# GRU chunks without zeroing: reset and keep inputs in a chunk's first step, candidate scan into PSUM

## The chip, the cores and the metric

The kernel runs on one core of a Trainium2 chip. The metric is the device time of one execution in microseconds (us), as the median of several runs. TensorE is called PE here, its weight loads PEld, VectorE is DVE, ScalarE is ACT, GpSimd is POOL.

## The reference

The network has four layers on an input of 8 x 16 x 16 x 96: a spectral mixing layer with an MLP, a Toeplitz layer, and two GRU layers (L2 and L3). The change concerns the GRU layers only. Each of them runs four independent GRUs (two sums of a forward and a reverse direction) over the 256 positions of the image, for 8 batch elements, with 96 hidden units. The recurrence cannot be split over the positions:

```python
def step(hprev, gxt):                 # gx = x @ wih.T + bih for all positions beforehand
    gh = hprev @ whh.T + bhh
    r = jax.nn.sigmoid(gxt[:, :h] + gh[:, :h])
    z = jax.nn.sigmoid(gxt[:, h:2 * h] + gh[:, h:2 * h])
    n = jnp.tanh(gxt[:, 2 * h:] + r * gh[:, 2 * h:])
    hn = (1.0 - z) * n + z * hprev
    return (hn, hn)
...
fwd = _bigru(x_inner, f_wih_fw, f_whh_fw, ...)
bwd = jnp.flip(_bigru(jnp.flip(x_inner, 1), b_wih_fw, b_whh_fw, ...), 1)
y = jax.nn.silu(fwd + bwd) * jax.nn.silu(z)
```

## The kernel before

`gru_steps` runs the 256 steps of a layer; it is called once for L2 and once for L3. The four GRUs form two groups g = 0 and 1 of two GRUs each (j = 0, 1); a group's state is 96 partitions (hidden units) by 16 columns (2 GRUs x 8 batch elements, `PER`). The loop over steps q does group 0 and then group 1 on every engine, so one group's step is a **half step**, and the two groups take turns. Every engine works through its own list in the order in which the code writes it; semaphores tie the lists together.

The state is kept as fp32 (`states`), and for PE as two fp16 parts, `h_hi` (rounded) and `h_lo` (the rest); the weights are two fp16 parts as well. A half step on PE is 12 small matmuls with `h_hi` (4 for each of the gates RESET, CAND, KEEP) and 6 with `h_lo` (2 for each gate), each with 8 moving columns. They add into PSUM sums that already hold the input's part.

Steps go in chunks of 8 (`STEPS`), 32 chunks a layer. The input's part of a gate, for all 8 steps of a chunk, takes 6 matmuls of 64 columns, called **products** here (`inputs`, line 1087, run at line 1105). Before the change the products of the next chunk are spread over the steps of the current one (`ahead`): one RESET and one KEEP product in six of the steps 1 to 7, six CAND products over all 8. RESET and KEEP have one bank for each group, which holds two chunks' regions (p = 0, 1), so the region of the next chunk is zeroed first, by ACT, in the first step of a chunk (lines 1077 and 1078), for 30 of the 32 chunks; the products then add onto zeros. CAND has a bank for each p, and its first product clears the bank (start=True).

A half step on the other engines: ACT takes the sigmoid of the RESET sum (line 1072), of the KEEP sum (`keep`, 1074), and of its negative (`renew`, 1075); in a chunk's first step it then writes the zeros. DVE's scan (1022, `cand`) computes input plus r times the hidden part; ACT takes its tanh (1081); DVE multiplies keep and the old state (1029, `kept_part`), and a scan gives the new `h_hi` (1037) and another one the fp32 state (1039), from which `h_lo` comes (1045, `rest`). DVE's list for one half step of group 0 is

```python
candidate(0, q)
rest(1, q - 1)
kept_part(0, q)
new_state(0, q)      # h_hi, then states
```

and for group 1 the same with the groups changed: the `h_lo` of one group stands behind the candidate of the other one.

## Time and profile before

| | |
|---|---|
| median of 3 runs | 1226.55 us (1225.07 to 1228.66) |
| the profiled execution | 1223.94 us |
| its span, first to last instruction | 1222.1 us |
| PE, DVE, ACT busy | 1081.0, 943.3, 777.5 us |
| granted TensorE clock, mean of the span | 0.585 |
| steps of L2, first to last candidate scan | 297.22 to 722.75 us |
| steps of L3, first to last candidate scan | 772.11 to 1197.45 us |

The profile counts matmuls as busy while they overlap, so that PE's busy time is not its work. The steps of the two GRU layers hold 851 us of the span. A granted clock of 1.0 is 2.4 GHz, 0.5 is 1.2 GHz.

### The profile page before, as it was taken

How to read it: one execution, taken by the hardware profiler on the slowest of the kernel's cores; microseconds unless marked ns; L12 is line 12 of the kernel's file. 1: busy time of each engine (PE TensorE's matmuls, PEld its weight loads, DVE VectorE, ACT ScalarE, POOL GpSimd, SP SyncE). 2: the span in 40 equal slices, each digit the busy share in tenths (PEclk: the TensorE clock that was granted, in tenths of full speed). 3: DMA queues.
4: the chain of work that ended last, by engine and by line, in shares of the span. 5: the costliest groups of instructions: out<-in, count | busy, mean ns of one | idle time of the engine just before them, and what ended most of it. 6: DMA issues, size and time to landing. Idle time of an engine off the chain costs nothing. (4 is left out here: it accounts for less than half of the span.)

```text
span 1222.1 us, 57375 instructions
## 1 busy us (share of the span) xinstructions
PE 1081.0 (88%) x22390; PEld 854.9 (70%) x22390; DVE 943.3 (77%) x5701; ACT 777.5 (64%) x4509; POOL 113.1 (9%) x94
## 2 busy tenths in 40 slices
PE   3787799858999999999999968999999999999996
PEld 2555254344888888888888855688888888888885
DVE  3544799984888888888888885688888888888886
ACT  4224620007777777777777764777777777777773
POOL 1001389910000000000000000000000000000000
PEclk8588899957555555555555557555555555555555
DMA  4000500000000000000000000000000000000000
GB/s 119 2 1 12 131 1 1 1 5 2 4 4 4 4 4 4 4 4 4 3 4 4 4 3 5 3 4 4 3 4 4 4 4 3 4 4 4 4 3 27
DMA packets 8234, 12.71 MB, mean 10 GB/s; under 512 B 5745, under 2 KB 7121, under 8 KB 7674
## 3 DMA queue, kind: packets, MB, share of 16 engines
q1 hardware_dynamic: 7962, 9.05, 2.9%
q8 instruction: 175, 2.87, 1.0%
q14 instruction: 97, 0.79, 0.2%
HBM read 8.26 MB, written 0.79 MB: 7 GB/s over the span
## 5 line engine op out<-in xcount | busy, mean ns | idle before, releaser
L1037 DVE TENSOR_TENSOR_SCAN L2s_h_hi<-L2s_renew,L2s_terms 96x32 f16<-96x32 f32 x512 | 112.9, 221 | 74.4 <-ACT L2s_terms L1081 16.0
L1037 DVE TENSOR_TENSOR_SCAN L3s_h_hi<-L3s_renew,L3s_terms 96x32 f16<-96x32 f32 x512 | 113.0, 221 | 74.4 <-ACT L3s_terms L1081 16.0
L1129 PE MATMUL L2s_reset_sum<-L2s_h_hi,L_w_hidden 97*128 97x8 f16 x2048 | 141.0, 179 | 20.8 <-DVE L2s_h_hi L1037 8.4
L1129 PE MATMUL L3s_reset_sum<-L3s_h_hi,L_w_hidden 97*128 97x8 f16 x2048 | 141.1, 179 | 20.6 <-DVE L3s_h_hi L1037 7.8
L1129 PEld LDWEIGHTS L3s_reset_sum<-L3s_h_hi,L_w_hidden 97*128 97x128 f16 x2048 | 94.6, 107 | 78.6 <-DVE L3s_h_hi L1037 31.5
L1129 PEld LDWEIGHTS L2s_reset_sum<-L2s_h_hi,L_w_hidden 97*128 97x128 f16 x2048 | 94.6, 107 | 78.6 <-DVE L2s_h_hi L1037 32.0
L1072 ACT ACTIVATE L3s_reset<-L3s_reset_sum 96x16 f32<-96x16 f32 x512 | 93.0, 182 | 65.8 <-PE L3s_reset_sum L1129 5.1
L1072 ACT ACTIVATE L2s_reset<-L2s_reset_sum 96x16 f32<-96x16 f32 x512 | 93.0, 182 | 65.7 <-PE L2s_reset_sum L1129 4.6
L1081 ACT ACTIVATE L2s_terms<-L2s_cand 96x16 f32<-96x16 f32 x512 | 111.0, 217 | 30.1 <-DVE L2s_cand L1022 3.5
L1129 PE MATMUL L3s_keep_sum<-L3s_h_hi,L_w_hidden 97*128 97x8 f16 x2048 | 130.0, 174 | 0.0
L1129 PE MATMUL L2s_keep_sum<-L2s_h_hi,L_w_hidden 97*128 97x8 f16 x2048 | 130.0, 174 | 0.0
L1129 PE MATMUL L3s_cand_sum<-L3s_h_hi,L_w_hidden 97*128 97x8 f16 x2048 | 130.0, 174 | 0.0
L1129 PE MATMUL L2s_cand_sum<-L2s_h_hi,L_w_hidden 97*128 97x8 f16 x2048 | 130.0, 174 | 0.0
L1081 ACT ACTIVATE L3s_terms<-L3s_cand 96x16 f32<-96x16 f32 x512 | 111.0, 217 | 29.6 <-DVE L3s_cand L1022 2.4
L1129 PE MATMUL L2s_reset_sum<-L2s_h_lo,L_w_hidden 96*128 96x8 f16 x1024 | 114.1, 185 | 0.8 <-DVE L2s_h_lo L1045 0.2
L1129 PE MATMUL L3s_reset_sum<-L3s_h_lo,L_w_hidden 96*128 96x8 f16 x1024 | 114.2, 185 | 0.7 <-DVE L3s_h_lo L1045 0.3
L1022 DVE TENSOR_TENSOR_SCAN L2s_cand<-L2s_reset,L2s_cand_sum 96x32 f32<-96x32 f32 x512 | 109.8, 214 | 3.0 <-ACT L2s_reset L1072 1.1
L1129 PE MATMUL L2s_keep_sum<-L2s_h_lo,L_w_hidden 96*128 96x8 f16 x1024 | 112.1, 183 | 0.0
L1129 PE MATMUL L3s_keep_sum<-L3s_h_lo,L_w_hidden 96*128 96x8 f16 x1024 | 112.1, 183 | 0.0
L1022 DVE TENSOR_TENSOR_SCAN L3s_cand<-L3s_reset,L3s_cand_sum 96x32 f32<-96x32 f32 x512 | 109.8, 214 | 2.8 <-ACT L3s_reset L1072 1.1
L692 DVE SCALAR_TENSOR_TENSOR l_acc<-l_v,coef,l_acc 96x384 f32<-96x384 f32 (+11 forms) x88 | 103.6, 1241 | 0.4
L1129 PE MATMUL L3s_cand_sum<-L3s_h_lo,L_w_hidden 96*128 96x8 f16 x1024 | 102.8, 174 | 0.0
(251 smaller groups left out, 3415.2 us busy)
## 6 DMA issues: line engine op xcount, KB each, us to landing
L_wih_raw<-in_L_wih SPq DMA_DIRECT2D x2, 1152.0 KB, 11.6
l_w_raw<-in_L_w SPq DMA_DIRECT2D x1, 1296.0 KB
L_w_hidden_raw<-in_L_whh SPq DMA_DIRECT2D x2, 576.0 KB
stream<-in_x SPq DMA_DIRECT2D x2, 384.0 KB, 3.7
out<-stream SPq DMA_DIRECT2D x4, 192.0 KB, 2.1
l_idft<-in_idft SPq DMA_DIRECT2D x1, 400.0 KB
rpe_lw<-in_rpe_lw SPq DMA_DIRECT2D x1, 384.0 KB
l_dft<-in_dft SPq DMA_DIRECT2D x1, 288.0 KB, 3.0
```

Of the source, the lines that this page charges most:

```text
L692: e.scalar_tensor_tensor(out=row(to, acc), in0=row(of, v), scalar=coef[:, m, axis, at:at + 1], in1=row(to, acc), op0=ALU.mult, op1=ALU.add ...
L1022: e.tensor_tensor_scan(flat(cand[g][:, x]), flat(reset[g][:, x]), flat(cand_sum(g, p)[0:C, :, :, s]), 0.0, ALU.mult, ALU.add).then_inc(can ...
L1037: e.tensor_tensor_scan(flat(h_hi[g][0:C, x]), flat(renew[g][:, x]), flat(terms[g][:, x]), 0.0, ALU.mult, ALU.add).then_inc(hi_ready[g], 1)
L1072: e.activation(reset[g][:, x, :, 1], reset_sum(g, p)[0:C, :, s], ACT.Sigmoid).then_inc(activated[g], 1)
L1081: e.activation(terms[g][:, x, :, 0], cand[g][:, x, :, 1], ACT.Tanh).then_inc(activated[g], 1)
L1129: return e.matmul(dst, weights.hidden[0:rows, wp, GATES * (2 * g + j) + gate, :], rhs, start=False, stop=False, skip_group_check=True)
```

## The change

The zeroing is gone, and with it the buffer `zeros`. RESET and KEEP use one region of their bank. All 6 RESET products and all 6 KEEP products of a chunk are run in the chunk's own first step, among the matmuls of the state; the first of each six has start=True and clears the bank's flags, so that the others and the state's matmuls write or add as is due. The KEEP matmuls with `h_hi` move behind the RESET and CAND matmuls with `h_lo`, in every step. The six CAND products of the next chunk stay spread over the steps. The candidate scan writes its result to a free part of the CAND bank in PSUM instead of SBUF, and the tanh reads it there.

```diff
-        cand = pairs("cand", [C, 2, PER, 2])
...
-        zeros = sb("zeros", [C, PER, STEPS])
...
-        reset_sum = lambda g, p: reset_bank[g][:, p]
-        keep_sum = lambda g, p: keep_bank[g][:, p]
+        reset_sum = lambda g, p: reset_bank[g][:, 0]
+        keep_sum = lambda g, p: keep_bank[g][:, 0]
...
+        cand = lambda g, p, x: cand_bank[g][p][0:C, 2].rearrange("p c s -> p (c s)")[:, x * 2 * PER:(x + 1) * 2 * PER]
...
-                    e.tensor_tensor_scan(flat(cand[g][:, x]), flat(reset[g][:, x]), flat(cand_sum(g, p)[0:C, :, :, s]), 0.0,
+                    e.tensor_tensor_scan(cand(g, p, x), flat(reset[g][:, x]), flat(cand_sum(g, p)[0:C, :, :, s]), 0.0,
                                          ALU.mult, ALU.add).then_inc(cand_ready[g], 1)
...
-                    renewed = s == 0 and 1 <= q // STEPS < CHUNK_COUNT - 1
...
-                        if renewed:
-                            e.activation(reset_sum(g, 1 - p)[0:C], zeros[:], ACT.Copy)
-                            e.activation(keep_sum(g, 1 - p)[0:C], zeros[:], ACT.Copy)
...
-                        e.activation(terms[g][:, x, :, 0], cand[g][:, x, :, 1], ACT.Tanh).then_inc(activated[g], 1)
+                        e.activation(terms[g][:, x, :, 0], cand(g, p, x).rearrange("p (c k) -> p c k", k=2)[:, :, 1], ACT.Tanh).then_inc(activated[g], 1)
...
-                            first = j == 0 and (wp, xp) == (0, 0) and (gate == CAND or chunk == 0)
+                            first = j == 0 and (wp, xp) == (0, 0)
...
-                        def ahead(gate, first):
-                            if following < CHUNK_COUNT:
-                                for product in share(inputs(g, gate, following), s, first):
-                                    run(product)
-
-                        e.wait_ge(hi_ready[g], q + 1)
-                        for gate in (RESET, CAND, KEEP):
+                        def high(gate):
                             for j in range(2):
                                 add(gate, 0, 0, j)
                                 add(gate, 1, 0, j)
-                        ahead(RESET, 1)
+
+                        e.wait_ge(hi_ready[g], q + 1)
+                        resets, keeps = (inputs(g, RESET, q // STEPS), inputs(g, KEEP, q // STEPS)) if s == 0 else ([], [])
+                        for product in resets[:1]:
+                            run(product)
+                        high(RESET)
+                        for product in resets[1:]:
+                            run(product)
+                        high(CAND)
 
                         e.wait_ge(lo_ready[g], q + 1)
                         add(RESET, 0, 1, 0)
                         add(RESET, 0, 1, 1).then_inc(reset_summed[g], 1)
                         add(CAND, 0, 1, 0)
                         add(CAND, 0, 1, 1).then_inc(cand_summed[g], 1)
-                        ahead(KEEP, 1)
+                        for product in keeps[:1]:
+                            run(product)
+                        high(KEEP)
+                        for product in keeps[1:]:
+                            run(product)
                         add(KEEP, 0, 1, 0)
                         add(KEEP, 0, 1, 1).then_inc(keep_summed[g], 1)
-                        ahead(CAND, 0)
+                        if following < CHUNK_COUNT:
+                            for product in share(inputs(g, CAND, following), s):
+                                run(product)
```

The order of PE's matmuls in a half step. `L2s_h_hi` and `L2s_h_lo` are the state's parts, `L_forward` is the input (its rows are the products), and x4 means four such matmuls in a row. In the first step of chunk 1 (step 8), group 0, PE has before the change:

```order
L1129 MATMUL L2s_reset_sum<-L2s_h_hi,L_w_hidden 128x8 x4
L1129 MATMUL L2s_cand_sum<-L2s_h_hi,L_w_hidden 128x8 x4
L1129 MATMUL L2s_keep_sum<-L2s_h_hi,L_w_hidden 128x8 x4
L1129 MATMUL L2s_reset_sum<-L2s_h_lo,L_w_hidden 128x8 x2
L1129 MATMUL L2s_cand_sum<-L2s_h_lo,L_w_hidden 128x8 x2
L1129 MATMUL L2s_keep_sum<-L2s_h_lo,L_w_hidden 128x8 x2
L1105 MATMUL L2s_cand_sum<-L_forward,L_w_input 128x8x8
```

and after it, at the same place:

```order
L1101 MATMUL L2s_reset_sum<-L_forward,L_w_input 128x64
L1122 MATMUL L2s_reset_sum<-L2s_h_hi,L_w_hidden 128x8 x4
L1101 MATMUL L2s_reset_sum<-L_forward,L_w_input 128x64 x5
L1122 MATMUL L2s_cand_sum<-L2s_h_hi,L_w_hidden 128x8 x4
L1122 MATMUL L2s_reset_sum<-L2s_h_lo,L_w_hidden 128x8 x2
L1122 MATMUL L2s_cand_sum<-L2s_h_lo,L_w_hidden 128x8 x2
L1101 MATMUL L2s_keep_sum<-L_forward,L_w_input 128x64
L1122 MATMUL L2s_keep_sum<-L2s_h_hi,L_w_hidden 128x8 x4
L1101 MATMUL L2s_keep_sum<-L_forward,L_w_input 128x64 x5
L1122 MATMUL L2s_keep_sum<-L2s_h_lo,L_w_hidden 128x8 x2
L1101 MATMUL L2s_cand_sum<-L_forward,L_w_input 128x8x8
```

Twelve products have moved into this half step, six of them ahead of the `h_lo` matmuls of RESET and six between those and the last KEEP matmul. In another step (step 7, group 1) there stands before:

```order
L1129 MATMUL L2s_reset_sum<-L2s_h_hi,L_w_hidden 128x8 x4
L1129 MATMUL L2s_cand_sum<-L2s_h_hi,L_w_hidden 128x8 x4
L1129 MATMUL L2s_keep_sum<-L2s_h_hi,L_w_hidden 128x8 x4
L1105 MATMUL L2s_reset_sum<-L_forward,L_w_input 128x64
L1129 MATMUL L2s_reset_sum<-L2s_h_lo,L_w_hidden 128x8 x2
L1129 MATMUL L2s_cand_sum<-L2s_h_lo,L_w_hidden 128x8 x2
L1105 MATMUL L2s_keep_sum<-L_forward,L_w_input 128x64
L1129 MATMUL L2s_keep_sum<-L2s_h_lo,L_w_hidden 128x8 x2
L1105 MATMUL L2s_cand_sum<-L_forward,L_w_input 128x8x8
```

and after:

```order
L1122 MATMUL L2s_reset_sum<-L2s_h_hi,L_w_hidden 128x8 x4
L1122 MATMUL L2s_cand_sum<-L2s_h_hi,L_w_hidden 128x8 x4
L1122 MATMUL L2s_reset_sum<-L2s_h_lo,L_w_hidden 128x8 x2
L1122 MATMUL L2s_cand_sum<-L2s_h_lo,L_w_hidden 128x8 x2
L1122 MATMUL L2s_keep_sum<-L2s_h_hi,L_w_hidden 128x8 x4
L1122 MATMUL L2s_keep_sum<-L2s_h_lo,L_w_hidden 128x8 x2
L1101 MATMUL L2s_cand_sum<-L_forward,L_w_input 128x8x8
```

The RESET and KEEP products have left, and the four KEEP matmuls with `h_hi` have moved from ahead of the `h_lo` matmuls to behind four of them. On ACT the first step of chunk 1, group 0, is before:

```order
L1072 ACTIVATE L2s_reset<-L2s_reset_sum 96x16
L1074 ACTIVATE L2s_keep<-L2s_keep_sum 96x16
L1075 ACTIVATE L2s_renew<-L2s_keep_sum 96x16
L1077 ACTIVATE L2s_reset_sum<-L2s_zeros 96x128
L1078 ACTIVATE L2s_keep_sum<-L2s_zeros 96x128
L1081 ACTIVATE L2s_terms<-L2s_cand 96x16
```

and after, with the next half step's first operation:

```order
L1071 ACTIVATE L2s_reset<-L2s_reset_sum 96x16
L1073 ACTIVATE L2s_keep<-L2s_keep_sum 96x16
L1074 ACTIVATE L2s_renew<-L2s_keep_sum 96x16
L1077 ACTIVATE L2s_terms<-L2s_cand_sum 96x16
L1071 ACTIVATE L2s_reset<-L2s_reset_sum 96x16
```

The two zeroing writes between `renew` and the tanh are gone, and the tanh reads the CAND bank.

## Rows read from the trace of the kernel before

**Rows 1.** The page: engine PE over the span, and the granted clock in 40 slices.

```profile
PE 1081.0 (88%) x22390; PEld 854.9 (70%) x22390; DVE 943.3 (77%) x5701; ACT 777.5 (64%) x4509; POOL 113.1 (9%) x94
...
PEclk8588899957555555555555557555555555555555
```

**Rows 2.** Busy time by window, the steps of L2; columns PE, PEld, DVE, ACT, POOL, clock.

```profile
310.00:720.00 410.00, 389.66 (x9944) 331.97 (x9942) 335.27 (x2461) 319.13 (x2089) 0.00 (x0) 0.50 0.02 4
```

**Rows 3.** Timeline, one ordinary half step: start us, duration us, engine, line, operation.

```profile
438.75 0.22 DVE L1022 TENSOR_TENSOR_SCAN L2s_cand<-L2s_reset,L2s_cand_sum 96x32 f32<-96x32 f32 x1
...
438.88 0.15 DVE L1045 TENSOR_TENSOR L2s_h_lo<-L_states,L2s_h_hi 96x16 f16<-96x16 f32 x1
...
439.00 0.22 ACT L1081 ACTIVATE L2s_terms<-L2s_cand 96x16 f32<-96x16 f32 x1
...
439.09 0.22 PE L1129 MATMUL L2s_reset_sum<-L2s_h_lo,L_w_hidden 96*128 96x8 f16 x2
...
439.25 0.22 DVE L1037 TENSOR_TENSOR_SCAN L2s_h_hi<-L2s_renew,L2s_terms 96x32 f16<-96x32 f32 x1
439.35 0.18 ACT L1072 ACTIVATE L2s_reset<-L2s_reset_sum 96x16 f32<-96x16 f32 x1
439.39 0.19 DVE L1039 TENSOR_TENSOR_SCAN L_states<-L2s_renew,L2s_terms 96x32 f32<-96x32 f32 x1
...
439.52 0.27 PE L1129 MATMUL L2s_reset_sum<-L2s_h_hi,L_w_hidden 97*128 97x8 f16 x4
439.56 0.22 DVE L1022 TENSOR_TENSOR_SCAN L2s_cand<-L2s_reset,L2s_cand_sum 96x32 f32<-96x32 f32 x1
...
439.86 0.21 PE L1105 MATMUL L2s_reset_sum<-L_forward,L_w_input 97*128 97x64 f16 x1
...
439.90 0.22 PE L1129 MATMUL L2s_reset_sum<-L2s_h_lo,L_w_hidden 96*128 96x8 f16 x2
```

**Rows 4.** Timeline of DVE: two candidate scans twelve half steps apart within a chunk.

```profile
446.24 0.22 DVE L1022 TENSOR_TENSOR_SCAN L2s_cand<-L2s_reset,L2s_cand_sum 96x32 f32<-96x32 f32 x1
...
456.00 0.22 DVE L1022 TENSOR_TENSOR_SCAN L2s_cand<-L2s_reset,L2s_cand_sum 96x32 f32<-96x32 f32 x1
```

**Rows 5.** Timeline, DVE and ACT, the first step of a chunk.

```profile
443.63 0.22 DVE L1022 TENSOR_TENSOR_SCAN L2s_cand<-L2s_reset,L2s_cand_sum 96x32 f32<-96x32 f32 x1
443.66 0.28 ACT L1077 ACTIVATE L2s_reset_sum<-L2s_zeros 96x128 f32<-96x128 f32 x1
...
444.06 0.21 ACT L1081 ACTIVATE L2s_terms<-L2s_cand 96x16 f32<-96x16 f32 x1
...
444.45 0.19 DVE L1039 TENSOR_TENSOR_SCAN L_states<-L2s_renew,L2s_terms 96x32 f32<-96x32 f32 x1
...
444.56 0.19 DVE L1022 TENSOR_TENSOR_SCAN L2s_cand<-L2s_reset,L2s_cand_sum 96x32 f32<-96x32 f32 x1
...
445.43 0.22 DVE L1022 TENSOR_TENSOR_SCAN L2s_cand<-L2s_reset,L2s_cand_sum 96x32 f32<-96x32 f32 x1
```

**Rows 6.** Groups by line and form: count, busy us, mean ns of one.

```profile
L1081 ACT ACTIVATE L2s_terms<-L2s_cand 96x16 f32<-96x16 f32 x512 | 111.0, 217 | 30.1 <-DVE L2s_cand L1022 3.5
...
L1072 ACT ACTIVATE L2s_reset<-L2s_reset_sum 96x16 f32<-96x16 f32 x512 | 93.0, 182 | 65.7 <-PE L2s_reset_sum L1129 4.6
```

**Rows 7.** Timeline of PE in the steps: two small matmuls, product, two small, product.

```profile
440.79 0.20 PE L1129 MATMUL L2s_cand_sum<-L2s_h_lo,L_w_hidden 96*128 96x8 f16 x2
440.84 0.21 PE L1105 MATMUL L2s_keep_sum<-L_forward,L_w_input 97*128 97x64 f16 x1
440.87 0.23 PE L1129 MATMUL L2s_keep_sum<-L2s_h_lo,L_w_hidden 96*128 96x8 f16 x2
440.95 0.21 PE L1105 MATMUL L2s_cand_sum<-L_forward,L_w_input 97*128 97x64 f16 x1
```

**Rows 8.** Timeline of PE, six products in a row before the first step.

```profile
294.73 0.34 PE L1105 MATMUL L2s_reset_sum<-L_forward,L_w_input 97*128 97x64 f16 x6 [0.94 <-PEq L892]
294.91 0.34 PE L1105 MATMUL L2s_cand_sum<-L_forward,L_w_input 97*128 97x64 f16 x6
```

More of the change, by code:

```diff
@@ L993, in gru_steps @@
         updated, hi_ready, lo_ready = each("updated"), each("hi_ready"), each("lo_ready")
-        PREPARED = 2 + 7 * GROUPS
+        PREPARED = 1 + 7 * GROUPS
         with nc.Block() as block:
@@ L1001, in _ @@
                 e.memset(warm[:], 0.0).then_inc(prepared, 1)
-                e.memset(zeros[:], 0.0).then_inc(prepared, 1)
                 for g in range(GROUPS):
@@ L1105, in run, with share @@
                     return e.matmul(dst, lhsT, rhs, start=start, stop=False, skip_group_check=True)
-                def share(products, s, first):
-                    if s < first:
-                        return []
-                    n, steps = len(products), STEPS - first
-                    return products[round((s - first) * n / steps):round((s - first + 1) * n / steps)]
+                def share(products, s):
+                    n = len(products)
+                    return products[round(s * n / STEPS):round((s + 1) * n / STEPS)]
                 for g in range(GROUPS):
-                    for gate in (RESET, CAND, KEEP):
-                        for product in inputs(g, gate, 0):
-                            run(product)
+                    for product in inputs(g, CAND, 0):
+                        run(product)
                 e.wait_ge(prepared, PREPARED)
@@ L1130, in add @@
                                             start=False, stop=False, skip_group_check=True)
-                        def ahead(gate, first):
-                            if following < CHUNK_COUNT:
-                                for product in share(inputs(g, gate, following), s, first):
-                                    run(product)
-                        e.wait_ge(hi_ready[g], q + 1)
-                        for gate in (RESET, CAND, KEEP):
+                        def high(gate):
                             for j in range(2):
@@ L1148, in _ @@
                         add(CAND, 0, 1, 1).then_inc(cand_summed[g], 1)
-                        ahead(KEEP, 1)
+                        for product in keeps[:1]:
[3 more added lines that the diff above has]
+                            run(product)
                         add(KEEP, 0, 1, 0)
                         add(KEEP, 0, 1, 1).then_inc(keep_summed[g], 1)
-                        ahead(CAND, 0)
+                        if following < CHUNK_COUNT:
+                            for product in share(inputs(g, CAND, following), s):
+                                run(product)
 def gru_output(nc, layer, stream, gate, states, w_out, w_loaded, stats, out_dram, stored):
```

## The prediction

> **What bounds the kernel now.** I read the page first: PE is busy 1081.0 of 1222.1 us, and its granted clock is 5 tenths through nearly all of the steps [rows 1]. The window over L2's steps says the same, 389.66 of 410 us busy at 0.50, that is the 1.2 GHz level [rows 2]. That looks like a kernel bound by PE, but matmuls overlap in the profile, so I went to the timeline of one half step [rows 3] and asked what each engine waits for.
>
> A chain closes there. The candidate scan starts at 438.75; `h_lo` of the other group stands right behind it, 438.88 to 439.03; PE starts its two RESET matmuls with `h_lo` at 439.09 and ends them at 439.31; ACT's sigmoid runs 439.35 to 439.53; the other group's candidate scan starts at 439.56. That is 0.81 us for a half step, through DVE, PE and ACT and back. Twelve half steps from 446.24 to 456.00 take 9.76 us, 0.813 each [rows 4], though by the code some hold a RESET and a KEEP product and some don't: the products now cost nothing.
>
> The other chain is slacker. The scan ends at 438.97, the tanh runs 439.00 to 439.22, the `h_hi` scan starts at 439.25, the state scan at 439.39 [rows 3]. A candidate scan that finds its data ready starts 0.11 us behind the state scan (444.45 to 444.56) [rows 5], so here it could have started at 439.50 and started at 439.56: slack 0.05 to 0.06 us. PE has slack too: it starts on `h_hi` at 439.52 and on `h_lo` at 439.90, 0.38 us later, and in between the 12 `h_hi` matmuls end their issue at 439.86, where a product fills the rest [rows 3].
>
> **What an ordinary step gains (7 of 8).** The products gone from it and the KEEP matmuls moved behind `h_lo` both leave PE idle where it now works in the shadow of `h_lo`; the RESET matmuls still wait for `h_lo`. Gain: 0. The move makes the KEEP sum later: behind the RESET sum come 2 CAND, 4 + 2 KEEP matmuls. Small matmuls start 0.027 us apart (two of them fill 440.79 to 440.84 [rows 7], and twelve, the first of them behind a wait, 439.52 to 439.86 [rows 3]), so KEEP is complete 8 x 0.027 = 0.21 us after RESET. RESET's sigmoid starts at 439.35, KEEP's then at 439.56, ends at 439.74; the multiplication of keep and state on DVE could start at 439.77, where `h_lo` of the other group (439.56 + 0.13 = 439.69, plus about 0.07) lets it start now anyway. What waits behind it is `h_hi`, 0.3 us later. Hidden; cost 0.
>
> The tanh from PSUM should be shorter: ACT's sigmoid from PSUM on the same 96x16 takes 182 ns, the tanh from SBUF 217 ns [rows 6]. I take 0.035 us. It lies on the slack chain, so in an ordinary step it is worth 0 and widens that slack from 0.055 to 0.09 us. The scan's write into PSUM has no row: no DVE operation of this kernel writes PSUM. Nearest rows: the candidate scan, which reads PSUM, takes 0.19 us when it waits for nothing, the state scan, SBUF only, 0.19 [rows 5]. I take 0 more. Up to 0.09 more in its latency is covered by the slack. The Trainium skill, "VectorE: DVE Perf Modes", section on the TRN2 errata, gives 58 cycles of fixed cost for SBUF to SBUF and 120 for PSUM to SBUF at 0.96 GHz, which would be 0.065 us more for PSUM; the trace disagrees for the read (0.19 against 0.19), and even 0.065 us would stay under the slack in an ordinary step, so that by that rule the sum below would hardly change.
>
> **What the zeroing costs now.** In a chunk's first step the two zero writes stand ahead of the tanh: it starts at 444.06, 0.43 us behind its scan instead of 0.25 [rows 3, 5]. The candidate scans go 443.63, 444.56, 445.43: 1.80 us for two half steps instead of 1.63. So 0.17 us a chunk; the condition `renewed` holds in 30 chunks of a layer. Gain: 2 layers x 30 x 0.17 = 10.2 us. That is all that there is to gain.
>
> **What the 12 products cost in the first step.** Price of one: product, two small matmuls, product start at 440.84, 440.87 and 440.95 [rows 7]; 0.11 us for one product and two small ones, so that with 0.027 for a small one a product takes 0.05 to 0.06; I take 0.053, its 64 columns at one a cycle of 1.2 GHz. At full clock six of them took 0.18 us, 0.030 each [rows 8]. Now the first step, with the steps of today as zero:
>
> 1. Group 0, RESET. From the start on `h_hi` to the start on `h_lo` PE has 8 small ones and 6 products: 0.21 + 0.32 = 0.53, and 0.02 for the slower start behind a wait (0.34 for the twelve of [rows 3], where 12 x 0.027 is 0.32), 0.55 instead of 0.38. The shorter tanh brings `h_hi` 0.035 earlier, and the second `h_lo` matmul, which now starts 0.05 after the first because that one waited, follows 0.02 sooner. Late by 0.17 - 0.055 = 0.12.
> 2. Group 1, RESET. It stands in PE's queue behind all of group 0: 4 small, 1 product, 4 small, 5 products, 2 small, 1 CAND product = 10 x 0.027 + 7 x 0.053 = 0.64, and then its own 0.53. 1.17 us behind group 0's instead of 0.81: late by another 0.36.
> 3. Next step of group 0. KEEP of group 1 is complete 8 x 0.027 + 6 x 0.053 = 0.53 behind its RESET. The candidate scan starts 0.21 behind the sigmoid of RESET [rows 3], the KEEP sigmoid 0.53 behind it: 0.32 after the scan. With 0.18 for it, 0.03 to DVE, 0.17 for the multiplication and 0.03 to the `h_hi` scan, that one starts 0.73 after the candidate scan instead of 0.50; the state scan 0.14 later; the next group's candidate 0.12 later, 0.99 instead of 0.81: late by another 0.18. This is the wait that is late next: DVE stands at KEEP with the other group's work queued behind it.
> 4. That candidate scan finds its sums ready and is 0.03 shorter: -0.03.
>
> Sum: 0.12 + 0.36 + 0.18 - 0.03 = 0.63 us a chunk, 32 chunks, 2 layers: +40.3 us. Against the 10.2: **+30 us**. One memset of zeros (96x128) less in each layer's start is under 0.2 us each. The profiled execution took 1223.94 us, so 1254 by this sum; the median of the runs stands 2.6 above it, so I predict **1256 us**.
>
> **Bounds.** Product price: at least that of a small matmul, 0.027, at most twice the full-clock one, 0.061. At 0.061 the sum grows by 0.008 x (6 + 13 + 6) = 0.2 a chunk, +13 us: 1269. At 0.027 steps 1 to 3 shrink to about 0.04 a chunk, 2.6 us less 10.2: 1219. The row 7 value is measured at this clock, so I keep 0.053. Tanh: no shorter, 0.035 x 64 = +2 us. Scan's latency: up to 0.09 more costs only in step 1, 64 x 0.09 = +6 us; beyond it each 0.01 costs 1024 half steps, 10 us.
>
> **The rivals.**
> - *The scan into PSUM holds DVE longer* (slower still). What counts is the 0.13 us from the scan's start to `h_lo` behind it [rows 3]: it is on the chain that closes. For: it reads and writes one bank. Against: reading PSUM alone shows no such cost. At 0.03 more: 1024 x 0.03 = +31 on top, 1287. Chance 0.10.
> - *The products cost less than I think* (other side): PE takes a product at the pace of its weight load. Then only the zeroing's gain is left: 1219. It decides from a price under about 0.034, where the sum of steps 1 to 3 falls under 0.16. Against it: [rows 7]. Chance 0.05.
> - *The clock rises* (other side). The first steps are dense runs of wide matmuls, and PE's granted clock before the steps was partly full [rows 1]. Products at 0.030 [rows 8] make it about 1219, and if it held through ordinary steps the two RESET matmuls with `h_lo` would be some 0.03 shorter and all half steps with them, down to 1190. Against: it stays at 0.50 with the same number of matmuls in the same time [rows 2]. The Trainium skill, "TensorE: Matmul & The Clock Gate", part 1, says that the throttle is the default and sustained activity releases it; by that rule the bursts speak for a rise, and this trace has PE busy 95% at half clock without one. Chance 0.05.
> - *PE or DVE make up part of it*, the groups shifting against each other so that steps 2 and 3 overlap: half of step 3 and a third of step 2 saved is 0.2 a chunk, 13 us less: 1243. Chance 0.18.
>
> **How the numbers follow.** The forecast itself, 0.62, is good for 1248 to 1265. To hold 8 in 10 I take in the partly made-up case and the start of the PSUM one: 1236 to 1275. A measurement of this kernel tells about 0.3%, 3.7 us. Faster: the two rivals of that side, 0.10, less a part that ends near zero: 0.09. Same: 0.04. Slower: 0.87.
>
> **What would show it.** Right: ordinary half steps still 0.81; no product between the ordinary matmuls; the two first half steps of a chunk and the next one some 0.9, 1.2 and 1.0 us; a tanh of about 0.18; in the first step the multiplication of keep and state late on DVE, and PE without a gap for two half steps at each chunk's start; the clock at 0.50. Wrong: ordinary half steps other than 0.81 (the scan's interval or the clock), or a first step that costs under 0.2 us (the product's price).

## The result and the profile after

The changed kernel takes 1270.89 us (median of 4 runs, 1268.7 to 1275.62); the kernel before took 1227.61 us beside it (4 runs, 1225.07 to 1228.67). The ratio is 1.0366, 95% interval 1.0347 to 1.0385: 43 us slower, where the sum of the prediction gave 30. The profiled execution took 1270.78 us, its span is 1269.0 us against 1222.1, and 44.7 of these 46.9 us lie between the first and the last candidate scan of the two layers: L2's steps now go from 297.51 to 745.25 us (447.7 instead of 425.5), L3's from 796.52 to 1244.33 (447.8 instead of 425.3). Of the 2.2 us outside the steps, 1.9 lie between the two layers (51.3 us instead of 49.4), where the granted clock is 0.63 instead of 0.67. That stretch takes 48.2 to 51.4 us in the eleven traces of this document, long and short ones with either order of the products, so these 1.9 us are not put down to the change.

The page of the changed kernel, PE's line and the granted clock, which answer to [rows 1]:

```profile
PE 1124.8 (89%) x22390; PEld 897.0 (71%) x22390; DVE 987.2 (78%) x5699; ACT 732.5 (58%) x4269; POOL 113.3 (9%) x94
...
PEclk8588899866555555555555556555555555555555
```

Busy time by window over L2's steps, the row that answers to [rows 2]:

```profile
310.00:720.00 410.00, 390.56 (x9492) 335.70 (x9489) 338.61 (x2338) 281.75 (x1871) 0.00 (x0) 0.50 0.01 4
```

PE does the same number of matmuls in the whole program, and its clock in the steps is 0.50 as before; in 410 us it now gets through 9492 instead of 9944. ACT has 240 instructions less. So less is done per microsecond by engines that look just as busy, and to see why one has to go to the half steps.

The timeline of DVE in the changed kernel, an ordinary half step (start, duration, in us), and two candidate scans twelve half steps apart, which answer to [rows 3] and [rows 4]:

```profile
446.62 0.22 DVE L1022 TENSOR_TENSOR_SCAN L2s_cand_sum<-L2s_reset,L2s_cand_sum 96x32 f32<-96x32 f32 x1
446.75 0.16 DVE L1045 TENSOR_TENSOR L2s_h_lo<-L_states,L2s_h_hi 96x16 f16<-96x16 f32 x1
...
447.10 0.22 DVE L1037 TENSOR_TENSOR_SCAN L2s_h_hi<-L2s_renew,L2s_terms 96x32 f16<-96x32 f32 x1
...
447.44 0.23 DVE L1022 TENSOR_TENSOR_SCAN L2s_cand_sum<-L2s_reset,L2s_cand_sum 96x32 f32<-96x32 f32 x1
...
455.00 0.22 DVE L1022 TENSOR_TENSOR_SCAN L2s_cand_sum<-L2s_reset,L2s_cand_sum 96x32 f32<-96x32 f32 x1
...
464.92 0.23 DVE L1022 TENSOR_TENSOR_SCAN L2s_cand_sum<-L2s_reset,L2s_cand_sum 96x32 f32<-96x32 f32 x1
```

Twelve half steps take 9.92 us, 0.827 each, where they took 9.76, 0.813 each. `h_lo` starts 0.13 us behind its scan as before, but it lasts 0.16 us. That is the closing chain, and it has become longer.

The first step of a chunk on DVE, answering to [rows 5]:

```profile
451.95 0.22 DVE L1022 TENSOR_TENSOR_SCAN L2s_cand_sum<-L2s_reset,L2s_cand_sum 96x32 f32<-96x32 f32 x1
...
452.48 0.17 DVE L1029 TENSOR_TENSOR L2s_terms<-L2s_keep,L_states 96x16 f32<-96x16 f32 x1 [0.24 <-ACT L2s_keep L1073]
452.76 0.22 DVE L1037 TENSOR_TENSOR_SCAN L2s_h_hi<-L2s_renew,L2s_terms 96x32 f16<-96x32 f32 x1
...
453.12 0.23 DVE L1022 TENSOR_TENSOR_SCAN L2s_cand_sum<-L2s_reset,L2s_cand_sum 96x32 f32<-96x32 f32 x1
...
454.19 0.20 DVE L1022 TENSOR_TENSOR_SCAN L2s_cand_sum<-L2s_reset,L2s_cand_sum 96x32 f32<-96x32 f32 x1
...
455.00 0.22 DVE L1022 TENSOR_TENSOR_SCAN L2s_cand_sum<-L2s_reset,L2s_cand_sum 96x32 f32<-96x32 f32 x1
```

The half steps here are 1.17 (451.95 to 453.12), 1.07 and 0.81 us (1.173, 1.064 and 0.817 in the median of the chunks); the one that ends at 451.95 took 0.94. PE in the same place:

```profile
450.94 0.23 PE L1101 MATMUL L2s_reset_sum<-L_forward,L_w_input 97*128 97x64 f16 x1
...
451.50 0.20 PE L1122 MATMUL L2s_reset_sum<-L2s_h_lo,L_w_hidden 96*128 96x8 f16 x2
...
452.11 0.24 PE L1101 MATMUL L2s_reset_sum<-L_forward,L_w_input 97*128 97x64 f16 x1
...
452.67 0.20 PE L1122 MATMUL L2s_reset_sum<-L2s_h_lo,L_w_hidden 96*128 96x8 f16 x2
```

From the first product to the first `h_lo` matmul there are 0.56 us, and from one group's `h_lo` to the other's 1.17. The groups of the changed kernel (count, busy us, mean ns of one), which answer to [rows 6] for the tanh:

```profile
L1022 DVE TENSOR_TENSOR_SCAN L2s_cand_sum<-L2s_reset,L2s_cand_sum 96x32 f32<-96x32 f32 x512 | 113.9, 222 | 8.7 <-ACT L2s_reset L1071 1.4 <-ACT L2s_keep L1073 1.1
...
L1077 ACT ACTIVATE L2s_terms<-L2s_cand_sum 96x16 f32<-96x16 f32 x512 | 93.3, 182 | 11.9 <-DVE L2s_cand_sum L1022 8.9
...
L1045 DVE TENSOR_TENSOR L2s_h_lo<-L_states,L2s_h_hi 96x16 f16<-96x16 f32 x512 | 81.4, 159 | 0.3
```

and two rows of the same view of the kernel before:

```profile
L1022 DVE TENSOR_TENSOR_SCAN L2s_cand<-L2s_reset,L2s_cand_sum 96x32 f32<-96x32 f32 x512 | 109.8, 214 | 3.0 <-ACT L2s_reset L1072 1.1 <-ACT L2s_keep L1074 0.9
...
L1045 DVE TENSOR_TENSOR L2s_h_lo<-L_states,L2s_h_hi 96x16 f16<-96x16 f32 x512 | 75.8, 148 | 0.3
```

The scan is 8 ns longer in the mean, and `h_lo` behind it 11 ns (medians 158 and 146), though `h_lo` itself reads and writes SBUF in both kernels. The tanh takes 182 ns instead of 217. The waits of the changed kernel (us in total, times, longest):

```profile
ACT L2s_reset L1071 <- PE L2s_reset_sum L1122: 92.1, 480, 0.8
...
ACT L2s_keep L1073 <- PE L2s_keep_sum L1122: 22.4, 64, 0.4
...
DVE L2s_terms L1029 <- ACT L2s_keep L1073: 14.8, 63, 0.2
```

ACT waits for KEEP 64 times in L2, once for each group and chunk, as step 3 of the prediction said, 0.35 us a time; DVE then waits for ACT 63 times, 0.24 us a time.

### The profile page after: what moved, and what is told of

It is laid out like the page before. It is cut to its first block and busy times, and to the rows that moved or that the text cites. A ratio compares the mean times of both kernels' runs of the same rounds, so it can differ in the third digit from the quotient of the medians.

```text
span 1269.0 us, 57133 instructions
## 1 busy us (share of the span) xinstructions
PE 1124.8 (89%) x22390; PEld 897.0 (71%) x22390; DVE 987.2 (78%) x5699; ACT 732.5 (58%) x4269; POOL 113.3 (9%) x94
## 5 line engine op out<-in xcount | busy, mean ns | idle before, releaser
L1122 PE MATMUL L3s_cand_sum<-L3s_h_hi,L_w_hidden 97*128 97x8 f16 x2048 | 131.8, 175 | 0.0
L1122 PE MATMUL L2s_cand_sum<-L2s_h_hi,L_w_hidden 97*128 97x8 f16 x2048 | 131.8, 175 | 0.0
L1122 PE MATMUL L3s_keep_sum<-L3s_h_hi,L_w_hidden 97*128 97x8 f16 x2048 | 131.6, 175 | 0.0
L1122 PE MATMUL L2s_keep_sum<-L2s_h_hi,L_w_hidden 97*128 97x8 f16 x2048 | 131.6, 175 | 0.0
L1122 PE MATMUL L3s_reset_sum<-L3s_h_lo,L_w_hidden 96*128 96x8 f16 x1024 | 111.9, 183 | 14.0 <-DVE L3s_h_lo L1045 2.0
L1122 PE MATMUL L2s_reset_sum<-L2s_h_lo,L_w_hidden 96*128 96x8 f16 x1024 | 111.9, 183 | 13.9 <-DVE L2s_h_lo L1045 2.0
L1122 PEld LDWEIGHTS L3s_reset_sum<-L3s_h_hi,L_w_hidden 97*128 97x128 f16 x2048 | 98.9, 109 | 31.4 <-DVE L3s_h_hi L1037 13.0
L1122 PEld LDWEIGHTS L2s_reset_sum<-L2s_h_hi,L_w_hidden 97*128 97x128 f16 x2048 | 98.8, 109 | 31.5 <-DVE L2s_h_hi L1037 13.0
L1022 DVE TENSOR_TENSOR_SCAN L3s_cand_sum<-L3s_reset,L3s_cand_sum 96x32 f32<-96x32 f32 x512 | 113.9, 222 | 8.8 <-ACT L3s_reset L1071 1.3
L1022 DVE TENSOR_TENSOR_SCAN L2s_cand_sum<-L2s_reset,L2s_cand_sum 96x32 f32<-96x32 f32 x512 | 113.9, 222 | 8.7 <-ACT L2s_reset L1071 1.4
L1073 ACT ACTIVATE L3s_keep<-L3s_keep_sum 96x16 f32<-96x16 f32 x512 | 92.2, 180 | 36.4 <-PE L3s_keep_sum L1122 22.4
L1073 ACT ACTIVATE L2s_keep<-L2s_keep_sum 96x16 f32<-96x16 f32 x512 | 92.2, 180 | 36.4 <-PE L2s_keep_sum L1122 22.4
L1122 PE MATMUL L3s_keep_sum<-L3s_h_lo,L_w_hidden 96*128 96x8 f16 x1024 | 104.5, 176 | 0.0
L1122 PE MATMUL L2s_keep_sum<-L2s_h_lo,L_w_hidden 96*128 96x8 f16 x1024 | 104.5, 176 | 0.0
```

Source lines behind the costliest of these rows:

```text
L1022: e.tensor_tensor_scan(cand(g, p, x), flat(reset[g][:, x]), flat(cand_sum(g, p)[0:C, :, :, s]), 0.0, ALU.mult, ALU.add).then_inc(cand_read ...
L1073: e.activation(keep[g][:, x], keep_sum(g, p)[0:C, :, s], ACT.Sigmoid).then_inc(activated[g], 1)
L1122: return e.matmul(dst, weights.hidden[0:rows, wp, GATES * (2 * g + j) + gate, :], rhs, start=False, stop=False, skip_group_check=True)
```

## The experiments

| kernel | us, median (range, runs) | ratio to before (95%) |
|---|---|---|
| before, all runs beside the changed kernel | 1227.61 (1225.07 to 1228.67, 4) | 1 |
| changed kernel | 1270.89 (1268.7 to 1275.62, 4) | 1.0366 (1.0347 to 1.0385) |
| 1: changed, scan to SBUF | 1263.41 (1260.05 to 1265.47, 4) | 1.0303 (1.0264 to 1.0341) |
| 2: before, scan to PSUM | 1237.37 (1235.59 to 1239.36, 4) | 1.0091 (1.0062 to 1.0119) |
| 3: before, KEEP matmuls moved | 1232.14 (1227.42 to 1234.48, 10) | 1.004 (1.0023 to 1.0057) |
| 4: changed, 10 of 12 products left out | 1228.99 (1225.25 to 1231.11, 10) | 1.002 (1.0004 to 1.0037) |
| 5: before, zero writes behind the tanh | 1224.35 (1219.79 to 1225.81, 12) | 0.9978 (0.9963 to 0.9992) |
| 6: changed, scan to another bank | 1270.85 (1267.52 to 1274.26, 4) | 1.0363 (1.033 to 1.0397) |
| 7: before, no zero writes | 1218.45 (1215.53 to 1219.56, 4) | 0.994 (0.9917 to 0.9963) |
| 8: experiment 5, `hi_ready` waited for first | 1217.99 (1212.36 to 1220.29, 6) | 0.9933 (0.9909 to 0.9957) |
| 9: changed, `updated` waited for first | 1272.25 (1267.84 to 1275.67, 6) | 1.0379 (1.0352 to 1.0406) |

Half steps below are distances between candidate scans in the profiled execution. The ratios are to runs of the kernel before that were made beside each experiment; their medians lie between 1224.72 and 1227.61 us. A difference by the steps of two profiled executions can be some 3 us off the one by the ratio, because the time outside the steps varies: the first candidate scan comes at 297.0 to 301.5 us in the eleven traces, and the stretch between the layers was given above.

### 1. Changed kernel, scan back to SBUF

```diff
+        cand_sb = pairs("cand", [C, 2, PER, 2])
-        cand = lambda g, p, x: cand_bank[g][p][0:C, 2].rearrange("p c s -> p (c s)")[:, x * 2 * PER:(x + 1) * 2 * PER]
+        cand = lambda g, p, x: flat(cand_sb[g][:, x])
```

> The changed kernel with one part undone: the candidate scan writes SBUF again, and the tanh reads SBUF. Theory A, the scan's write into PSUM makes each ordinary half step 0.827 instead of 0.813 us (h_lo behind it ends 0.158 after its start instead of 0.146): half steps go back to 0.813, 1022 x 0.0133 = 13.6 us less, some 2 us given back because the tanh takes 0.217 again in the first steps: 1259 us. Rival B, the longer ordinary half step comes from the KEEP matmuls that moved behind h_lo: half steps stay at 0.827, 1271 to 1273 us.

1263.41 us, ratio 1.0303: 7.5 us less than the changed kernel (8.3 by the steps of the two layers in the profile). The ordinary half step is 0.813 again, and `h_lo` lasts 148 ns:

```profile
L1046 DVE TENSOR_TENSOR L2s_h_lo<-L_states,L2s_h_hi 96x16 f16<-96x16 f32 x512 | 75.9, 148 | 0.3
```

This is 4 us more than expected. The expectation took 0.0133 us off each of the 1022 half steps, but only the 12 ordinary ones of a chunk get shorter (10.2 us); the two half steps that follow a chunk's first scan stay at 1.17 and 1.06 (PE's queue and the wait for KEEP set them, not `h_lo`), and the one ahead of them grows from 0.94 to 0.97, because the tanh is longer again (1.5 us). The rest of the loss, 37 us by the ratio and 36.4 by the steps of the two layers, comes from these three half steps, less what the zeroing had cost.

### 2. Kernel before, only the scan into PSUM

```diff
+        cand = lambda g, p, x: cand_bank[g][p][0:C, 2].rearrange("p c s -> p (c s)")[:, x * 2 * PER:(x + 1) * 2 * PER]
-                    e.tensor_tensor_scan(flat(cand[g][:, x]), flat(reset[g][:, x]), flat(cand_sum(g, p)[0:C, :, :, s]), 0.0,
+                    e.tensor_tensor_scan(cand(g, p, x), flat(reset[g][:, x]), flat(cand_sum(g, p)[0:C, :, :, s]), 0.0,
-                        e.activation(terms[g][:, x, :, 0], cand[g][:, x, :, 1], ACT.Tanh).then_inc(activated[g], 1)
+                        e.activation(terms[g][:, x, :, 0], cand(g, p, x).rearrange("p (c k) -> p c k", k=2)[:, :, 1], ACT.Tanh).then_inc(activated[g], 1)
```

> The kernel before with one part of the change alone: the candidate scan writes the CAND bank in PSUM, the tanh reads it there. Theory A: half steps of 0.826 us, +13 us, less about 0.03 us in each chunk's first step because the tanh is shorter: 1236 to 1241 us. Rival B (the scan is not the cause): half steps of 0.813 and a gain of 2 us by the shorter tanh in the first steps, 1226 us.

1237.37 us, ratio 1.0091, 11 us more (9.6 by the steps). Here too the ordinary half step is 0.827, and `h_lo`, from the same view:

```profile
L1045 DVE TENSOR_TENSOR L2s_h_lo<-L_states,L2s_h_hi 96x16 f16<-96x16 f32 x512 | 81.4, 159 | 0.3
```

Done alone and undone alone, the scan's result in PSUM costs 0.013 us in an ordinary half step. In both kernels the tanh is shorter by 35 ns and gives nothing back in an ordinary half step, since it is on the slack chain.

### 3. Kernel before, only the KEEP matmuls moved

```diff
-                        for gate in (RESET, CAND, KEEP):
+                        def high(gate):
...
+
+                        high(RESET)
+                        high(CAND)
...
+                        high(KEEP)
```

> The kernel before with one part of the change alone: KEEP's matmuls with h_hi stand behind the RESET and CAND matmuls with h_lo. My prediction says that this costs nothing in ordinary steps (0.813 us a half step) and up to 2 us in the first steps, where the zero writes now start later: 1228 to 1230 us. Rival: KEEP's later sum delays the keep product and with it h_hi in every step: half steps of 0.82 or more, 1235 us and up.

1232.14 us, ratio 1.004, 5 us slower, more than expected. Ordinary half steps are still 0.813, so the move costs nothing there, although it uses up slack: the `h_hi` scan starts 0.54 us behind the candidate scan instead of 0.50. The first step tells the rest; ACT in this kernel:

```profile
444.19 0.28 ACT L1077 ACTIVATE L2s_reset_sum<-L2s_zeros 96x128 f32<-96x128 f32 x1
444.39 0.27 ACT L1078 ACTIVATE L2s_keep_sum<-L2s_zeros 96x128 f32<-96x128 f32 x1
444.59 0.21 ACT L1081 ACTIVATE L2s_terms<-L2s_cand 96x16 f32<-96x16 f32 x1
```

The scan of this half step starts at 444.04. The zero writes stand behind the KEEP sigmoids, which are later now, so they start 0.15 us behind the scan instead of 0.03, and the tanh 0.55 instead of 0.43 [rows 5]. The two half steps take 1.04 and 0.82, 1.86 us instead of 1.80: with 60 such steps 3.4 us, of 3.8 by the steps of the two layers. In the changed kernel there are no zero writes, so this cost isn't in it.

### 4. Changed kernel, first products only

Ten of the twelve RESET and KEEP products of each chunk and group are left out, so that most of the input's part is missing from those gates.

```diff
-                        for product in resets[1:]:
-                            run(product)
...
-                        for product in keeps[1:]:
-                            run(product)
```

> The changed kernel with 10 of the 12 RESET and KEEP products of a chunk left out (only the first one of each gate, which clears the bank, is run), so that input parts are missing from the sums. Theory: the burst of products is what costs; without it a chunk's first step falls from 2.23 to about 1.65 us and the time to about 1228 us (the zeroing's gain of 10 less the 13 of the scan). Rival: the first step is long because PE waits for semaphores or because of the clearing of the bank; then it stays above 1.9 us and the time above 1245.

1228.99 us, ratio 1.002. L2's steps take 426.8 us instead of 447.7, L3's 426.8 instead of 447.8: the ten products cost 42.0 us, nearly the whole of what was lost. The first step's half steps are 0.83 like all others, and DVE no longer waits for KEEP. What is left over the kernel before, 2.7 us by the steps, is the scan's cost in every half step less what the zeroing had cost.

### 5. Kernel before, zero writes behind the tanh

RESET's region is zeroed in step 0 and KEEP's in step 1 of a chunk, each behind the tanh, where ACT otherwise waits for the next RESET sum; PE gets a wait for them.

```diff
-                    renewed = s == 0 and 1 <= q // STEPS < CHUNK_COUNT - 1
+                    renewed = s < 2 and 1 <= q // STEPS < CHUNK_COUNT - 1
...
-                        if renewed:
-                            e.activation(reset_sum(g, 1 - p)[0:C], zeros[:], ACT.Copy)
-                            e.activation(keep_sum(g, 1 - p)[0:C], zeros[:], ACT.Copy)
...
+                        if renewed:
+                            e.activation((reset_sum, keep_sum)[s](g, 1 - p)[0:C], zeros[:], ACT.Copy).then_inc(zeroed[g], 1)
...
+                        if s in (1, 2) and 1 <= q // STEPS < CHUNK_COUNT - 1:
+                            e.wait_ge(zeroed[g], 2 * (q // STEPS - 1) + s)
                         e.wait_ge(hi_ready[g], q + 1)
...
-                        ahead(KEEP, 1)
+                        ahead(KEEP, 2)
```

> A version that should beat both: the kernel before, products spread as there, but ACT writes the zeros behind the tanh, where it is idle, RESET's in a chunk's first step and KEEP's in its second; PE waits for them at the start of the next step of that group, and KEEP's products start a step later. Theory: a zero write takes 0.2 us of ACT and ACT has about 0.28 us between the tanh's issue and the next sigmoid, so it is hidden: all half steps 0.813, 10 us less than before, 1217 us. Rival: PE's extra wait or the next sigmoid pays for it, a first step of 1.7 us or more, 1222 us or more.

1224.35 us, ratio 0.9978: a small gain, not the 10 us. The step with the zero write behind the tanh is fine, 0.813 each. Late are the half steps behind the new wait, 0.88 once for step 1 and once for step 2. ACT, DVE and PE there:

```profile
447.01 0.26 ACT L1080 ACTIVATE L2s_reset_sum<-L2s_zeros 96x128 f32<-96x128 f32 x1
...
447.14 0.22 DVE L1037 TENSOR_TENSOR_SCAN L2s_h_hi<-L2s_renew,L2s_terms 96x32 f16<-96x32 f32 x1
...
447.50 0.26 PE L1128 MATMUL L2s_reset_sum<-L2s_h_hi,L_w_hidden 97*128 97x8 f16 x4
```

PE starts 0.36 us behind the start of the `h_hi` scan instead of 0.27 [rows 3], although the zero write it also waits for had ended at 447.27. The trace has an instruction that only waits, by itself, on PE at 447.40, and it bears the line of the second of the two waits, `hi_ready`:

```profile
L1138 PEldq EVENT_SEMAPHORE  x242: 51/51/51, 299.7 to 1174.8; - x121
```

It is in the row 51 ns long, and the matmul follows it. This led to experiment 8.

### 6. Changed kernel, scan into another bank than it reads

```diff
-        cand = lambda g, p, x: cand_bank[g][p][0:C, 2].rearrange("p c s -> p (c s)")[:, x * 2 * PER:(x + 1) * 2 * PER]
+        cand = lambda g, p, x: reset_bank[g][0:C, 2].rearrange("p c s -> p (c s)")[:, x * 2 * PER:(x + 1) * 2 * PER]
```

> The changed kernel, but the candidate scan writes a free part of the group's RESET bank instead of the CAND bank that it reads. Theory C, the 0.013 us come from DVE reading and writing one and the same PSUM bank: half steps of 0.813, about 1258 us. Theory D, they come with any DVE write into PSUM: half steps of 0.827 and 1271 us, as the changed kernel.

1270.85 us, ratio 1.0363. The groups:

```profile
L1022 DVE TENSOR_TENSOR_SCAN L2s_reset_sum<-L2s_reset,L2s_cand_sum 96x32 f32<-96x32 f32 x512 | 113.9, 222 | 8.2 <-ACT L2s_reset L1071 1.2 <-ACT L2s_keep L1073 1.1
...
L1045 DVE TENSOR_TENSOR L2s_h_lo<-L_states,L2s_h_hi 96x16 f16<-96x16 f32 x512 | 81.4, 159 | 0.3
```

Same durations, same time: it is not that one bank is read and written at once, which the prediction's rival had for its reason.

In every run in which the scan writes PSUM the tanh also reads it there, so the tanh's read is a rival. The changed kernel's first step settles it:

```profile
451.95 0.22 DVE L1022 TENSOR_TENSOR_SCAN L2s_cand_sum<-L2s_reset,L2s_cand_sum 96x32 f32<-96x32 f32 x1
...
452.09 0.16 DVE L1045 TENSOR_TENSOR L2s_h_lo<-L_states,L2s_h_hi 96x16 f16<-96x16 f32 x1
...
452.41 0.18 ACT L1077 ACTIVATE L2s_terms<-L2s_cand_sum 96x16 f32<-96x16 f32 x1
```

Here the tanh starts 0.16 us after the end of `h_lo`, and `h_lo` still lasts 0.158 us in the median of these half steps, against 0.146 at the same place in experiment 1. So it is the scan's write. Why the operation behind the scan is the one that pays is not shown.

### 7. Kernel before without the zero writes

The two zero writes are left out: from the third chunk on, the products add onto old sums.

```diff
-                        if renewed:
-                            e.activation(reset_sum(g, 1 - p)[0:C], zeros[:], ACT.Copy)
-                            e.activation(keep_sum(g, 1 - p)[0:C], zeros[:], ACT.Copy)
```

> The kernel before without the zero writes of ACT, so that the sums of later chunks add onto old ones (the computation is changed). It prices the part that the change can gain: 0.17 us in the first step of 30 chunks in each layer, 10.2 us, 1217 us, and no first step longer than the others. Rival: PE, not ACT, holds the first step; then the time stays at 1227.

1218.45 us, ratio 0.994; L2's steps are 5.3 us shorter and L3's 5.1. All that the zeroing costs is 10.4 us by the steps and 7 (5 to 10) by the ratio; of the gap between them 2 us are the stretch between the layers, 51.4 us in this profile and 49.4 before.

### 8. Experiment 5 with the two waits in the other order

```diff
+                        e.wait_ge(hi_ready[g], q + 1)
                         if s in (1, 2) and 1 <= q // STEPS < CHUNK_COUNT - 1:
                             e.wait_ge(zeroed[g], 2 * (q // STEPS - 1) + s)
-                        e.wait_ge(hi_ready[g], q + 1)
```

> The kernel before with the zero writes behind the tanh, as in the fifth experiment (RESET's region in the chunk's step 0, KEEP's in step 1, PE waiting for `zeroed`), but on PE the wait for `hi_ready` is now written ahead of the wait for `zeroed`. In the trace of the fifth experiment the only thing late was PE's start on h_hi in the two half steps that hold both waits: the second written wait had become a semaphore instruction of its own (51 ns), and since the awaited `hi_ready` was the one on it, the first matmul started 0.09 us later than behind a single wait. Theory 'the wait that comes last stands on an instruction of its own': with the order turned round `hi_ready` is on the matmul itself, all half steps of steps 0 to 2 are 0.813, each period of a chunk's first two steps 1.627 instead of 1.70 to 1.73, and the whole kernel gains what it gains without any zero write: 10 us less than before, 1217, ratio 0.992. Rival 'the zero write on ACT itself delays the next RESET sigmoid, or PE's first matmul behind it': the half steps of 0.88 stay, 1224, ratio 0.998.

1217.99 us, ratio 0.9933 (0.9909 to 0.9957), 8 us faster than before by the ratio and 10.3 by the steps, and as fast as the kernel without any zero write. DVE and PE at the same place of the program:

```profile
446.67 0.22 DVE L1037 TENSOR_TENSOR_SCAN L2s_h_hi<-L2s_renew,L2s_terms 96x32 f16<-96x32 f32 x1
...
446.94 0.28 PE L1128 MATMUL L2s_reset_sum<-L2s_h_hi,L_w_hidden 97*128 97x8 f16 x4
```

0.27 us again, and all half steps of steps 0 to 2 are 0.813. L2's steps take 420.2 us, L3's 420.4, against 420.3 and 420.2 without zero writes. The zero write of 0.26 us fits behind the tanh at no cost. This version beats both kernels.

### 9. Changed kernel, the multiplication waited for first

```diff
+                    e.wait_ge(updated[g], 2 * q + 1 + BEFORE[g])
                     e.wait_ge(activated[g], 3 * q + 3)
-                    e.wait_ge(updated[g], 2 * q + 1 + BEFORE[g])
```

> The changed kernel, but in the new_state function of DVE the wait for `updated` (the multiplication of keep and state) is written ahead of the wait for `activated` (the tanh). Nothing else. Theory 'second wait on an instruction of its own': in a chunk's first step the late one, `updated`, is now on the h_hi scan itself, which then starts 0.03 instead of 0.10 us behind the end of the multiplication: the second and third half steps of a chunk are 0.03 to 0.07 shorter in the chain that passes there, the third 0.99 instead of 1.06, 64 x 0.07 = 4.5 us less in all, 1266, ratio to before about 1.033. In ordinary steps the tanh is now the one on the extra instruction: h_hi 0.07 later, which the slack of 0.09 just covers, 0.8265 stays. Rival 'the 0.07 belongs to the multiplication's write, whatever the order': nothing changes, 1271. Second rival, the other sign: the extra 0.07 in every ordinary step is more than the slack, and each 0.01 over it costs 10 us: 1275 or more, h_hi and all half steps later.

DVE in the first step of a chunk:

```profile
454.22 0.17 DVE L1029 TENSOR_TENSOR L2s_terms<-L2s_keep,L_states 96x16 f32<-96x16 f32 x1 [0.23 <-ACT L2s_keep L1073]
454.43 0.22 DVE L1037 TENSOR_TENSOR_SCAN L2s_h_hi<-L2s_renew,L2s_terms 96x32 f16<-96x32 f32 x1
...
454.86 0.23 DVE L1022 TENSOR_TENSOR_SCAN L2s_cand_sum<-L2s_reset,L2s_cand_sum 96x32 f32<-96x32 f32 x1
...
455.86 0.20 DVE L1022 TENSOR_TENSOR_SCAN L2s_cand_sum<-L2s_reset,L2s_cand_sum 96x32 f32<-96x32 f32 x1
```

The `h_hi` scan starts 0.21 us behind the start of the multiplication instead of 0.28 (452.48 to 452.76 above), and the third half step is 1.00 instead of 1.06: the price of a wait on an instruction of its own is confirmed, 0.06 to 0.07 us. Ordinary half steps stay 0.827. But the time is 1272.25 us, ratio 1.0379, the same as that of the changed kernel, where I expected 4.5 us less. The half step before a chunk's first scan grew from 0.94 to 0.99: there the tanh, now the one on the extra instruction, is on the chain that closes (it leads to `h_hi` and to PE's six products), and what step 3 wins, step 1 loses. The expectation had reckoned with ordinary half steps only. The two theories about the mechanism are told apart by this run; the forecast of the time was wrong.

## Why the prediction came out as it did

The direction held, and so did the mechanism of the first step; that of the ordinary half step did not, and the sum was 13 us too small. The median lies in the upper part of 1236 to 1275, and one run, 1275.62, outside. That the range held is in part luck: it reached up for the start of the PSUM rival, and the sum itself held nothing for it. By the profiled steps it is 44.7 instead of 30.1 us. Point by point:

- **Ordinary half steps: gain 0, 0.813 stays.** Wrong, and the main error. The products and the moved KEEP matmuls cost and gain nothing there, as said (experiment 3). The failing step is "I take 0 more" for the scan's write into PSUM. The cost is 0.0133 us, 12 half steps a chunk and 64 chunks: 10.2 us. The nearest rows had been the scan that reads PSUM and the one that doesn't; that reading is free said nothing of writing. And "Up to 0.09 more in its latency is covered by the slack" looked at the tanh, which indeed stayed in its slack; what lengthened was the operation behind the scan on DVE, which is on the closing chain. The first rival named exactly this place, at 0.03 and with a chance of 0.10; its reason (one bank) was wrong (experiment 6), its size more than twice too large, and it reckoned with all 1024 half steps where 768 pay.
- **The zeroing is worth 10.2 us.** Right: 10.4 by the steps (experiment 7), 7 by the ratio.
- **The tanh 0.035 shorter, hidden.** Right, 182 ns. But in the changed kernel it brings the ordinary `h_hi` scan only from 0.500 to 0.486 us behind the candidate scan: with the KEEP matmuls moved the multiplication ends at 0.383 instead of 0.368 (experiment 2), and 0.10 us for its wait make the 0.486, later than the tanh, which ends at 0.440 and needs 0.03. In experiment 2 the `h_hi` scan starts at 0.473. This is worked out from the medians of the traces; no run tests it.
- **Step 1, +0.12.** Measured 0.94 - 0.813 = 0.13. **Step 2, +0.36.** Measured 1.173 - 0.813 = 0.36; PE's 0.56 and 1.17 us are the 0.55 and 1.17 of the sum, and with them the product's price of 0.053 at this clock. Experiment 4 gives 42.0 us for ten of the products where the four steps summed to 40.3.
- **Step 3, +0.18.** The wait for KEEP and its place were right: the KEEP sigmoid starts 0.32 us behind the scan, the multiplication at 0.53, both as predicted. The `h_hi` scan was put at 0.73 and came at 0.81, because the wait for the multiplication is an instruction of its own and costs 0.10 from the end of it to the scan where I took 0.03. The step is 0.25: 0.07 x 64 = 4.5 us more (experiment 9 shows 0.06 of it).
- **Step 4, -0.03.** Measured +0.003. The scan that finds its sums ready is 0.026 shorter, but what closes the chain is the end of `h_lo`, 0.285 us behind the scan's start, where an ordinary half step of the kernel before has 0.283. So nothing is gained: 0.033 x 64 = 2.1 us more. The write into PSUM costs nothing that shows in this half step: with the scan in SBUF (experiment 1) it takes the same 0.815.
- **What stays.** 10.2 for the scan, 4.5 for step 3, 2.1 for step 4 and 0.4 for step 1, less 0.2 for the zeroing, make 17.0, and 14.6 were missing. Both kernels have irregular long half steps, 0.05 to 0.3 us over the usual one at their place in the chunk: 36 of the 511 of a layer before, 17 after. All that departs from the usual half step of its place, with the two chunks of a layer that have no zeroing taken at 0.813, sums to 9.2 us before and 6.7 after over both layers, 2.5 less, which leaves 0.1 us. Many of the long ones recur every 128 half steps, as numbers 118, 246, 374 and 502 (counted from 0) of L2 in both kernels. In number 118 before, which starts at 395.31, DVE starts the `h_hi` scan at 396.14, though the tanh and the multiplication that it needs had ended by 395.78. What holds it up is open, and with it why the changed kernel has fewer.
- **The other rivals.** The products are not cheap, the clock stayed at 0.50, and nothing of steps 2 and 3 was made up by the groups' shifting: 1.173 and 1.064 recur in chunk after chunk.

PE gets runs of some 60 matmuls without a gap at each chunk's start (450.94 to 453.26), and the granted clock of the steps stays at 0.50, the 1.2 GHz level. The Trainium skill, "TensorE: Matmul & The Clock Gate", part 1, says that activity releases the throttle, which had spoken for a rise; the steps of all eleven traces show 0.50.

The Trainium skill, "VectorE: DVE Perf Modes", section Specifications, says that VectorE sits closer to SBUF and ScalarE closer to PSUM. By that rule a VectorE write into PSUM should take longer and a ScalarE read from it less; the traces agree, with 8 to 12 ns more on DVE and 35 ns less on ACT. The page gives no price for the write.

## What to carry to other kernels

In a recurrence two chains close in turns: before an intermediate result is put into another memory, see which chain each of the two engines stands on, since a reader that is 35 ns faster in the slack gives nothing and a writer that makes the chain 13 ns longer is paid in every ordinary half step, 768 times here. Work that fills gaps for free when it is spread is paid in full when it is bunched ahead of a wait, once for each group that is queued behind it; here the twelve products of each group cost nothing when spread and, for both groups together, 0.7 us a chunk when bunched. And where an instruction waits for two semaphores, write first the wait that comes last on the chain that closes, after seeing in every kind of step which one that is: that order alone was worth 5.5 us by the ratios and 7.9 by the steps between experiments 5 and 8, with the work moved to a free place on ACT and not away.

## What was not expected of the hardware

- A DVE scan that writes PSUM lasts 222 instead of 214 ns, and the DVE operation behind it, with all its operands in SBUF, starts no later but lasts 158 instead of 146 ns (medians). It is the same whether the bank is the one that the scan reads or another. Behind a scan that finds its data ready the write costs nothing that shows (`h_lo` ends 0.285 us after the scan's start with the write into PSUM, 0.286 without, experiment 1).
- The second of two waits ahead of an instruction is an instruction of its own (21 ns on DVE, 51 ns on PE). If the semaphore on it comes last, what follows starts 0.06 to 0.07 us later on DVE and 0.09 us later on PE than if that semaphore is on the instruction itself; if it comes early, it costs nothing that shows. The Trainium skill, "Perfetto Trace Analysis", section Identifying Dependency Chains, says that instructions which wait on several engines may have semaphore instructions put ahead of them; the traces agree, with these lengths, and the page has no price.
- A DVE scan that finds its data ready is 0.026 us shorter than one that waited, but the operation behind it ends no earlier in the kernel before (0.284 against 0.283 us after the scan's start) and only 0.010 us earlier in the changed one (0.285 against 0.295).
